# The first w1 product of expert 4 goes to PSUM bank 6 and no longer waits for the SiLU behind the exponentials

## The reference, cut to what matters

```python
scores = einsum('bhtd,bhsd->bhts', q, k) / sqrt(HD); scores = where(causal, scores, -1e30)
att = softmax(scores, axis=-1)
y = einsum('bhts,bhsd->bhtd', att, v)
x = x + y @ wo.T
flat = _rmsnorm(x, ln2_w)
weights = top-2 gate of softmax(flat @ router_w.T)
for e in range(NE):
    hh = silu(flat @ w1[e].T) * (flat @ w3[e].T)
    out = out + weights[:, e:e + 1] * (hh @ w2[e].T)
return x + out
```

## Time and profile before

| | us |
|---|---|
| median of 3 runs | 7286.18 (7277.96 to 7286.59) |
| the profiled execution | 7289.36 |
| its span | 7287.6 |
| TensorE busy | 6652.6 (91% of the span) |
| VectorE busy | 4615.7 (63%) |
| ScalarE busy | 4417.5 (61%) |

### The profile page before, as it was taken

How to read it: one execution, slowest core, us unless ns; L and a number is a source line. 1 busy time by engine, 2 the same in 40 slices (tenths; PEclk the granted TensorE clock), 3 DMA queues, 4 the chain that set the end, 5 groups by cost and what they waited for, 6 DMA issues and landing times. The chain is left out here.

```text
span 7287.6 us, 138653 instructions
## 1 busy us (share of the span) xinstructions
PE 6652.6 (91%) x43858; PEld 4057.5 (56%) x43858; DVE 4615.7 (63%) x7185; ACT 4417.5 (61%) x8385; POOL 3746.7 (51%) x1364
## 2 busy tenths in 40 slices
PE   8999899999899999899999899999999578888888
PEld 3444566666666666666666544444444255555555
DVE  8999577777477776577776333333333477777774
ACT  5666467667467666576675577777777444444443
POOL 8999277787278786377875244444444100000000
PEclk9999999999899999999999999999999778888888
DMA  2333455554555554555554311111111333333330
GB/s 98 111 114 112 173 164 166 167 166 159 179 166 167 167 169 157 182 166 167 166 166 166 105 54 48 48 48 53 49 48 48 105 80 75 75 75 75 74 75 3
DMA packets 595494, 835.11 MB, mean 115 GB/s; under 512 B 450408, under 2 KB 491496, under 8 KB 529768
## 3 DMA queue, kind: packets, MB, share of 16 engines
q1 hardware_dynamic: 595432, 834.33, 36.8%
HBM read 477.60 MB, written 356.58 MB: 114 GB/s over the span
## 5 line engine op out<-in xcount | busy, mean ns | idle before, releaser
L958 POOL TENSOR_TENSOR sb_rstd<-sb_var,sb_minus_half 128x16 f32<-128x16 f32 x1280 | 3690.1, 2899 | 2008.9 <-DVE sb_var L909 1010.9
L700 DVE TENSOR_TENSOR sb_unit<-H,sb_rstd 128x512 f32<-128x512 f32 x768 | 528.8, 688 | 684.4 <-POOL sb_rstd L958 546.2
L517 PE MATMUL H<-sb_conv_block,sb_act_in 128*128 128x128 f32 x6144 | 826.4, 283 | 8.8 <-DVE sb_unit L700 6.8
L517 PEld LDWEIGHTS H<-sb_conv_block,sb_act_in 128*128 128x128 f32 x6144 | 732.6, 192 | 124.6 <-issue 115.4
L622 ACT ACTIVATE sb_act_px<-sb_unit 128x512 f32<-128x512 f32 x768 | 483.9, 630 | 493.0 <-DVE sb_unit L706 492.9
L2328 POOL TENSOR_TENSOR blk_pos<-blk_pos,blk_mag 128x260 f32<-128x260 f32 x32 | 23.0, 738 | 1311.7 <-ACT blk_mag L1983 1311.7
L645 ACT ACTIVATE sb_act_out<-TC 128x512 f32<-128x512 f32 x768 | 447.7, 583 | 181.9 <-PE TC L532 181.9
L921 DVE COPY sb_act_out<-TC 128x512 f32<-128x512 f32 x256 | 176.9, 691 | 595.4 <-PE TC L767 595.4
L784 PE MATMUL M<-sb_dense,sb_fc_w 128*64 128x512 f32 x2048 | 521.5, 608 | 30.5 <-ACT sb_dense L867 25.5
L703 DVE TENSOR_TENSOR sb_unit<-sb_unit,sb_gain_row 128x512 f32<-128x512 f32 x768 | 531.4, 692 | 26.2
L706 DVE TENSOR_TENSOR sb_unit<-sb_unit,sb_shift_row 128x512 f32<-128x512 f32 x768 | 531.3, 692 | 26.1
(11 more groups left out here) (276 smaller groups left out, 12765.2 us busy)
## 6 DMA issues: line engine op xcount, KB each, us to landing
act_scratch<-sb_act_out SPq DMA_DIRECT2D x256, 1024.0 KB, 3.9
sb_act_in<-act_scratch SPq DMA_DIRECT2D x256, 1024.0 KB, 5.3
spectrum_in<-sb_f_sb SPq DMA_DIRECT2D x512, 78.0 KB, 1.8
sb_x_in<-spectrum_in SPq DMA_DIRECT2D x48, 832.0 KB, 4.4
spectrum_out<-sb_y_sb SPq DMA_DIRECT2D x48, 832.0 KB, 4.6
sb_z_in<-spectrum_out SPq DMA_DIRECT2D x512, 78.0 KB, 5.1
blk_rows_b<-scan_rows SPq DMA_DIRECT2D x128, 260.0 KB, 6.4
blk_rows_bb<-scan_rows SPq DMA_DIRECT2D x128, 260.0 KB, 7.4
```

What stands on the lines that cost most here:

```text
L517: e.matmul(H[j][:, 128 * u:128 * u + 128], act_in[p][:, 128 * b:128 * b + 128], conv_block[:, :], start=(u == 0), stop=False, skip_group_c ...
L700: e.tensor_tensor(rows, H[k][:, :].rearrange("p (y c) -> p y c", c=C), rstd[k][:, :].unsqueeze(2).to_broadcast([128, 16, C]), ALU.mult).th ...
L958: e.tensor_tensor(rstd[j][:, :], var[j][:, :], minus_half[:, :], ALU.pow).then_inc(rstd_ready, 1)
```

## The change

A constant `AHEAD = EXP_AFTER + 2 = 12` is added. In slot 12, and only there, the w1 product is written to bank 6 instead of bank 0, and the SiLU of slot 12 reads bank 6. Since bank 0 isn't written, the product waits for the SiLU of slot 10 instead of slot 11; and since bank 6 held scores, it waits until all masks of the group in attention have been added. Nothing else moves. Slot 13 writes bank 0 again and waits for the SiLU of slot 12 as before.

```diff
         EXP_AFTER = 10
+        AHEAD = EXP_AFTER + 2
...
                 if x < NE:
 
+                    if n == AHEAD and attn is not None:
+                        wait(e, "masked", attn)
                     if n > 0:
-                        wait(e, "silu", g, n)
-                    e.matmul(B[0][0:2 * HP, 0:TOK], expert("w1", x, k, 2 * HP), ue[:, :], start=True, stop=True)
+                        wait(e, "silu", g, n - 1 if n == AHEAD else n)
+                    e.matmul(B[6 if n == AHEAD else 0][0:2 * HP, 0:TOK], expert("w1", x, k, 2 * HP), ue[:, :], start=True, stop=True)
...
-                        e.activation(silu[n % 2][:, :], B[0][0:2 * HP, 0:TOK], ACT.Silu).then_inc(sig["silu"], 1)
+                        e.activation(silu[n % 2][:, :], B[6 if n == AHEAD else 0][0:2 * HP, 0:TOK], ACT.Silu).then_inc(sig["silu"], 1)
```

## The result

The changed kernel takes 7318.27 us (median of 5 runs, 7307.21 to 7330.69) against 7286.59 (7277.96 to 7295.14): a ratio of 1.0038, 95% interval 1.0026 to 1.0050. It is slower by 32 us, clear of noise. The profiled execution took 7313.69, its span is 7311.9, 24.3 us more than before.

What follows compares the result with a forecast made beforehand. VectorE was taken to set the pace up to slot 14, TensorE from there to slot 22. 32.5 - 12.2 - 2.5 = +17.8 on the profiled 7289.36 gave 7307.2, as a median 7304.0 us; range 7274 to 7320.

Steps and rivals of the forecast that it cites:

- The likeliest case: Whole kernel: slower through a late low clock behind slot 14, 7304 us, own range 7291 to 7316, chance 0.45.
- No change that can be told: Whole kernel: a difference within 0.2%, here 14.6 us; chance 0.47.
- The wait removed and what hides it: Slots 12 to 14: w1 starts early, other waits take over; direct gain 0.85 us in each of four windows.
- The added wait and the other bank: Slot 12: masks already done, anything below 1.5 us hidden; SiLU from bank 6 the same 0.39 us read.
- The clock: First parts (slot 12 to 22): clock falls behind slot 14 in all full windows, 35.80 us each, +32.5 in total.
- a sign of being wrong: Slots 12 and 13: the clock falling there as before would show the prediction wrong.
- Given back in the second part: Slot 22 to the next slot 12: shorter second parts give back 12.2 us, the middle of 0 and 24.3.
- The two last windows: Window without scan and window of experts alone: -2.5 us together, bounds -3 and 0.
- The sum: Whole kernel: 32.5 - 12.2 - 2.5 = +17.8 us, ends +5 and +36.5.
- A: Slots 12 to 14: clock falls where it fell, hidden by VectorE; -6 us, 7280, or 7286 without visible effect; chance 0.30.
- B: All windows: each takes the eighth window's rhythm, pitch 89.89 us; -18 us, 7268; chance 0.10.
- C: Second parts: nothing given back, they stay at 57.78 us; +30 us, 7316; chance 0.15.

Runs made afterwards that it cites:

- Experiment 5: Changed kernel plus unread TensorE products: three between w1 and w3 of slot 12, two behind its w2, six in slot 14; 7264.42 us, ratio 0.9974 to the kernel before.
- experiment 1: Changed kernel, but w1 of slot 12 waits for the SiLU of slot 11 again, still in bank 6; 7288.17 us, ratio 0.9998 to the kernel before.
- experiment 2: Kernel before plus five unread TensorE products in slot 12 ahead of the wait for the SiLU; 7316.94 us, ratio 1.0039.
- experiment 4: Kernel before plus five unread TensorE products in slot 12 and six between w1 and w3 of slot 14; 7270.59 us, ratio 0.9974.
- experiment 6: Kernel before plus unread TensorE products: five in slot 12, six in slot 14, twelve at the front of each window with a scan; 7227.09 us, ratio 0.9914.
- experiment 7: Kernel before plus only the twelve unread TensorE products at the front of each window with a scan; 7260.84 us, ratio 0.9959.

## Why the prediction was right

The waits, the place of the late fall of the clock and the sign came out as forecast. The closeness of the size is in part luck: windows without the late fall and windows with a longer one than forecast make up for each other. The likeliest case put the time at 7304 (7291 to 7316), and the median of 7318.27 is 2 us above that case's own range. "No change that can be told" had a slightly higher chance (0.47) than slower (0.43), so the forecast was not sure of the sign.

*The wait removed and what hides it.* Right in place and size: w3 of slot 12 is held by the hid of slot 10, w3 of slot 14 by VectorE, whose hid of slot 12 ends 11.01 us behind the last scan product of slot 12 as before. Experiment 5 shows no gain of the change at full clock either.

*The added wait and the other bank.* Right: cost nil, by experiment 1.

*The clock.* That the late low clock makes the loss is shown and not only argued: filling the early idle time, without taking away a wait, brings a loss of the same size (experiment 2); filling the late one too removes it and more (experiment 4). The mean was met: a first part of 35.72 against the 35.80 forecast, 14 x (35.72 - 33.47) = +31.4 us (forecast +32.5). The step to this mean was wrong in half of the windows. I had expected the fall behind slot 14 in every full window, with 3 us idle before it and full clock up to there. It comes in 11 of 14, with the long idle time in seven. In the other seven windows the clock is already low in slots 13 and 14, which the prediction had named as a sign of being wrong. In four of these it is low again or still behind slot 14: in windows 3, 5 and 10 it goes back to 1.00 for 3.4 us in between, in window 2 it stays at 0.50 for 17 us. The length of the late low clock was off too: in windows 9 and 12 it lasts 13.7 us and not 7, and the first parts are 37.86 and 38.64. Three first parts near 32.5 and four above 37 even out to the forecast mean; that is luck. What decides between the kinds was not found.

*Given back in the second part.* Second parts have a mean of 56.99 instead of 57.78, 13 x -0.79 = -10.3 (forecast -12.2, the middle of two ends).

*The two last windows.* From the last L1802 to the end it takes 7311.9 - 7164.71 = 147.2 instead of 148.0 us: -0.8, where I had -2.5. This term was mis-sized.

*The sum.* +31.4 - 10.3 - 0.8 = +20.3 from the first full window on, against +17.8. This window began 3.9 us later (5923.75 instead of 5919.81), ahead of any instruction that the change touches; in the other profiled kernels it begins between 5914.5 and 5928.7. Together that is 24.2, the difference of the spans (24.3) but for rounding. The medians differ by 31.7. The 7.4 us beyond lie in which executions were profiled: before 2.8 above its median, after 4.6 below. Why single executions of the changed kernel spread over 23 us was not followed up; the mixture of kinds of windows may be the cause, but only one execution is profiled and this is not shown. Two readings in the prediction are slightly off without touching its sum: the mean first part of before is 33.47, not 33.48, and it is the last nine slices of the clock that stand at 7 and 8, not seven.

*Rivals.* A (the clock falls where it fell and only there) happened in three windows of 14. B did not happen. C (nothing is given back) comes nearer to the median with its 7316 than the forecast with 7304, but not by its mechanism: in the profiled execution about a third of the first parts' loss was given back.

"TensorE: Matmul & The Clock Gate" of the Trainium skill, section "HAM oscillation — how this bites in real kernels", advises, for a kernel whose TensorE waits for transfers between groups of products, to restructure the loop so that it stays busy. No run here restructures a loop; what a busy TensorE is worth in this kernel shows in experiment 6: with its idle times at the front and in slots 12 and 14 filled by products that nobody needs, the kernel is 0.86% faster.

## What to carry to other kernels

Before a stall is removed, ask where the same idle time will turn up: if another engine sets the pace, the idle time only moves. For TensorE the place matters twice. Under another engine's time a low clock costs little (window 7 before: 9.6 us of it, first part 34.05, against 32.86 at full clock in experiment 4). Where TensorE sets the pace it is paid in full (window 3 before: 6.8 us of it, first part 36.09). Compare the granted clock of such stretches between iterations of the kernel at hand: two odd windows of the old trace had already shown what the change would do to half of them.

## What was not expected of the hardware

Products that nobody reads make the kernel faster, where the change made it 32 us slower: 12 at the front and 11 in slots 12 and 14 of each full window take 58 us off 7285. In window 7 before, the clock is low for the 9.6 us behind the stall of 2.59 us. In windows 8 to 14 of experiment 7 it is at 1.00 behind the same stall, and so it was in the third window of before, with this row:

```profile
6103.14 0.69 PE L1718 MATMUL bank<-blk_ue,blk_experts 128*114 128x260 f32 x2 [2.59 <-ACT blk_silu L2031]
```

The windows of an execution also fall into repeating patterns: before the change, first parts of 32.3, 32.9 and 34.05 by turns; with the front filled, seven windows in a row at 37.7.
